# Graph convolution on one core: order, biases and first layer of the edge MLP changed

## What is computed

```
h   = relu(layernorm(x));  xp = h @ lin1                      # [12500, 128]
C   = 0.5 * (cos(edge_weight * pi / 10) + 1)                  # [212500]
W   = (ssp(edge_attr @ w1 + b1) @ w2 + b2) * C[:, None]       # [212500, 128], ssp(v) = softplus(v) - log 2
agg = segment_sum(xp[src] * W, dst)                           # [12500, 128]
out = x + ssp(agg @ lin2 + lin2_b) @ lin + lin_b
```

## Time and profile before

| | us |
|---|---|
| median of 3 runs | 2164.73 |
| lowest, highest run | 2164.29, 2168.45 |
| span of the profiled execution | 2162.6 |
| TensorE matmul busy | 1804.4 (83%) |
| VectorE busy | 1433.5 (66%) |
| ScalarE busy | 636.2 (29%) |
| GpSimd busy | 1626.7 (75%) |

### The profile page before, as it was taken

One profiled execution on the slowest core, in us unless ns is written; L12 is line 12 of the kernel. 1 busy time (PEld: TensorE's weight loads), 2 busy tenths in 40 slices (PEclk: granted clock), 3 DMA queues, 4 the chain that ended last, 5 costly groups with the idle time before them and its releaser, 6 DMA issues.

```text
span 2162.6 us, 28443 instructions
## 1 busy us (share of the span) xinstructions
PE 1804.4 (83%) x8534; PEld 1331.3 (62%) x8535; DVE 1433.5 (66%) x3688; ACT 636.2 (29%) x976; POOL 1626.7 (75%) x1742
## 2 busy tenths in 40 slices
PE   6888888888877888878888888888878888878887
PEld 6556666666655656656665666666656666655665
DVE  7867666666665666666666666666667666666665
ACT  6323232222222222222232222222322223222221
POOL 7877777777777777777777777777777777777775
PEclk9678787687787787887687877777778678788776
DMA  9322222222232222223232222222222222232221
GB/s 286 90 73 69 81 76 75 79 76 81 68 82 81 71 79 81 75 74 82 68 82 79 77 79 70 81 81 68 81 81 75 74 81 76 74 81 76 73 72 47
DMA packets 100170, 175.95 MB, mean 81 GB/s; under 512 B 29163, under 2 KB 67748, under 8 KB 94870
## 3 DMA queue, kind: packets, MB, share of 16 engines
q0 software_dynamic: 53152, 108.91, 18.0%
q1 hardware_dynamic: 46868, 65.22, 11.4%
HBM read 161.21 MB, written 12.80 MB: 80 GB/s over the span
## 4 chain that ended last, share of the span: by engine, by line
POOL 60%; issue 20%; PE 14%; DMA 3%; DVE 2%; DVEq 0%; ACT 0%; POOLq 0%; SPq 0%
POOL XG L307 59%; PE PW L619 4%; PE PA L631 4%; PE PX L605 3%; DMA XG<-xp_scratch,IX 3%; PE PW L617 1%; DVE SCR L403 1%; POOL TB L207 1%; DVE XG L509 1%; PE PF L648 0%; DVE MV L409 0%; PE PF L656 0%; PE PW L586 0%; DMA X<-x 0%; PE PX L573 0%
## 5 line engine op out<-in xcount | busy, mean ns | idle before, releaser
L307 POOL DMA_INDIRECT XG<-xp_scratch,IX x1661 | 1574.8, 948 | 507.4 <-issue 498.3
L371 ACT ACTIVATE TB<-TB 128x512 f32<-128x512 f32 x416 | 261.7, 629 | 1407.0 <-DVE TB L491 1406.9
L619 PEld LDWEIGHTS PW<-W,TB 128*128 128x128 f32 x3322 | 592.2, 251 | 21.4
L619 PE MATMUL PW<-W,TB 128*128 128x128 f32 x3322 | 594.5, 338 | 0.0
L509 DVE TENSOR_TENSOR XG<-PW,XG 128x512 f32<-128x512 f32 x416 | 286.2, 688 | 451.1 <-DMA XG<-xp_scratch,IX 448.1
L605 PE MATMUL PX<-AT,W 50*128 50x512 f32 x832 | 554.8, 752 | 7.1 <-DMA AT<-attr_t 7.1
L631 PEld LDWEIGHTS PA<-OH,XG 128*128 128x128 f32 x3322 | 544.4, 248 | 1.0 <-DVE XG L509 0.5
L631 PE MATMUL PA<-OH,XG 128*128 128x64 f32 x3322 | 543.3, 322 | 0.2 <-DVE AG L517 0.2
L617 PEld LDWEIGHTS PW<-BPB,ones 128*128 128x128 bf16 x416 | 41.3, 99 | 704.4 <-issue 649.6
L617 PE MATMUL PW<-BPB,ones 128*128 128x512 bf16 x416 | 195.2, 469 | 315.4 <-DVE XG L509 314.4
L491 DVE TENSOR_SCALAR TB<-PX,B 128x512 f32<-128x512 f32 x416 | 309.8, 745 | 202.9 <-PE PX L605 200.5
(11 more groups left out here) (73 smaller groups left out, 329.2 us busy)
## 6 DMA issues: line engine op xcount, KB each, us to landing
AT<-attr_t SPq DMA_DIRECT2D x103, 400.0 KB
XG<-xp_scratch,IX POOLq DMA_INDIRECT x1661, 2.5
X<-x SPq DMA_DIRECT2D x12, 512.0 KB, 7.4
xp_scratch<-XG SPq DMA_DIRECT2D x24, 256.0 KB, 4.4
out<-X SPq DMA_DIRECT2D x24, 256.0 KB, 5.2
IX<-src_t SPq DMA_DIRECT2D x1, 830.5 KB, 6.5
CC<-ew_t SPq DMA_DIRECT2D x1, 830.5 KB, 8.4
DI<-dst_t SPq DMA_DIRECT2D x1, 830.5 KB
```

The source lines that it names most:

```text
L307: e.indirect_dma_start(XG[q % XG_N][0:p, k * D:(k + 1) * D], None, xp, bass.IndirectOffsetOnAxis(ap=IX[0:p, t0 + k:t0 + k + 1], axis=0)).t ...
L371: e.activation(T[:, 0:w], T[:, 0:w], ACT.Exp).then_inc(s_ex, 1)
L619: ins = e.matmul(P[0:p, k * D:(k + 1) * D], TB[q % TB_N][:, k * TILE:k * TILE + p], W2[:, :], start=False, stop=(k == n - 1))
```

## The change

- b1 is a 51st row of W1, against a row of ones in AT (`one`, loaded once per buffer). VectorE's clamp with b1 goes.
- ssp is written as max(v, 0) + Ln(0.5 exp(-|v|) + 0.5): ScalarE takes |v| from PSUM, then Exp and Ln, and VectorE adds.
- W1 and AT are laid out twice, on partitions 0 to 50 and 64 to 114. Even quads of a load lie below, odd ones above. At every even step TensorE runs the first layer of quads q and q+1, in halves of 256 columns that take turns between the two halves of its rows. `PX` has four banks.
- b2 is laid out over 128 partitions once (`BB`), and ScalarE copies it into `PW` ahead of the second layer (from quad 2 on), which then adds to it; the bf16 matmul goes.
- The masks of a quad are one instruction without C; C goes into the multiply, which becomes four instructions of 128 columns, each waiting for its own gather.
- `PA` is one bank. The accumulate of q moves to step q+4 of VectorE, ahead of the multiply of q+1, and the scatter of q waits for the accumulate of q-1.
- SP issues three table loads per turn in place of two, and two loads per attribute buffer in place of one.

```diff
--- before.py
+++ after.py
@@ -52,11 +53,12 @@
...
-    XG_N, TB_N, X1_N, OH_N = 6, 4, 3, 3
+    XG_N, TB_N, X1_N, OH_N = 6, 4, 4, 3
...
@@ -85,14 +87,14 @@
...
-        W1 = sb("W1", [NG, D])
+        W1 = sb("W1", [ODD + NG + 1, D])
...
-        B1 = sb("B1", [128, 2])
+        BB = sb("BB", [128, QT, D])
...
@@ -106,7 +108,7 @@
-        AT = [sb(f"AT{i}", [NG, CHQ * QE]) for i in range(AT_N)]
+        AT = [sb(f"AT{i}", [ODD + NG + 1, CHQ // 2 * QE]) for i in range(AT_N)]
...
@@ -118,9 +120,9 @@
-        PA = [ps(f"PA{i}") for i in range(2)]
+        PA = ps("PA")
-        PN = PW + PA
+        PN = PW + [PA, PX[3]]
...
@@ -239,28 +243,38 @@
...
             tables = [(IX[:, :], src_t, s_ix), (CC[:, :], ew_t, s_tb),
-                      (B1[:, 0:1], b1.rearrange("(p a) -> p a", a=1), s_bs),
...
-                      (W1[:, :], w1, s_dx), (W2[:, :], w2, s_dx), (WI[:, :], win, s_dx),
+                      (W1[0:NG, :], w1, s_dx), (W1[NG:NG + 1, :], b1.rearrange("(a d) -> a d", a=1), s_dx),
+                      (W1[ODD:ODD + NG, :], w1, s_dx),
+                      (W1[ODD + NG:ODD + NG + 1, :], b1.rearrange("(a d) -> a d", a=1), s_dx), (W2[:, :], w2, s_dx), (WI[:, :], win, s_dx),
                       (DUE, due.rearrange("(a q) -> a q", a=1), s_dx), (L2[:, :], lin2, s_dx), (L3[:, :], lin, s_dx)]
+            tables += [(AT[i][r + NG:r + NG + 1, :], one, s_dx) for i in range(AT_N) for r in (0, ODD)]
             for c in range(NNC):
                 keep(c)
                 if c >= 3 and c % 2 and tables:
-                    for _ in range(2):
+                    for _ in range(3):
...
-                e0 = k * CHQ * QE
-                w = min(CHQ * QE, EDGES - e0)
...
-                e.dma_start(AT[k % AT_N][:, 0:w], attr_t[:, e0:e0 + w]).then_inc(s_at[k % AT_N], 16)
+                for r in range(2):
+                    A = AT[k % AT_N][ODD * r:ODD * r + NG, :]
+                    if k < NCH - 1:
+                        e.dma_start(A.rearrange("p (j e) -> p j e", e=QE),
+                                    attr_t[:, k * CHQ * QE:(k + 1) * CHQ * QE].rearrange(
+                                        "p (j r e) -> p r j e", r=2, e=QE)[:, r]).then_inc(s_at[k % AT_N], 16)
+                    else:
+                        for j in range(CHQ // 2):
+                            e0 = (k * CHQ + 2 * j + r) * QE
+                            w = min(QE, EDGES - e0)
+                            e.dma_start(A[:, j * QE:j * QE + w], attr_t[:, e0:e0 + w]).then_inc(s_at[k % AT_N], 16)
...
@@ -361,16 +375,28 @@
...
+            e.wait_ge(s_bb, 1)
             for i in range(STEPS):
                 q = i
                 if q < NQ:
                     t0, n, last = quad(q)
                     w = (n - 1) * TILE + last
                     T = TB[q % TB_N]
-                    e.wait_ge(s_cl, q + 1)
-                    e.activation(T[:, 0:w], T[:, 0:w], ACT.Exp).then_inc(s_ex, 1)
+                    e.wait_ge(s_x1, q + 1)
+                    if q >= TB_N:
+                        e.wait_ge(s_w, q - TB_N + 1)
+                    e.activation(T[:, 0:w], PX[q % X1_N][:, 0:w], ACT.Abs).then_inc(s_ab, 1)
+                    e.wait_ge(s_ab, q + 1)
+                    e.activation(T[:, 0:w], T[:, 0:w], ACT.Exp, scale=-1.0).then_inc(s_ex, 1)
                     e.wait_ge(s_ex, q + 1)
                     e.activation(T[:, 0:w], T[:, 0:w], ACT.Ln, scale=0.5, bias=HALF[:, :]).then_inc(s_ln, 1)
+                q = i - 1
+                if 2 <= q < NQ:
+                    t0, n, last = quad(q)
+                    p = last if n == 1 else TILE
+                    e.wait_ge(s_m, q - 1)
+                    e.activation(PW[q % 2][0:p, 0:n * D], BB[0:p, 0:n, :].rearrange("p k d -> p (k d)"),
+                                 ACT.Copy).then_inc(s_pb, 1)
...
@@ -438,7 +464,8 @@
...
-            e.wait_ge(s_bs, 64)
+            e.wait_ge(s_bs, 48)
+            e.tensor_copy(BB[:, :, :], BR[:, 0, 0:1, :].to_broadcast([128, QT, D])).then_inc(s_bb, 1)
...
@@ -454,13 +481,12 @@
...
-            e.tensor_scalar_add(B1[:, 1:2], B1[:, 0:1], -LN2)
...
@@ -479,42 +505,38 @@
...
-                    e.scalar_tensor_tensor(out=T[:, 0:w], in0=PX[q % X1_N][:, 0:w], scalar=B1[:, 1:2],
-                                           in1=T[:, 0:w], op0=ALU.add, op1=ALU.max).then_inc(s_h, 1)
-                q = i
-                if q < NQ:
-                    t0, n, last = quad(q)
-                    w = (n - 1) * TILE + last
-                    e.wait_ge(s_x1, q + 1)
-                    if q >= TB_N:
-                        e.wait_ge(s_w, q - TB_N + 1)
-                    e.tensor_scalar(TB[q % TB_N][:, 0:w], PX[q % X1_N][:, 0:w], B1[:, 0:1], CLAMP,
-                                    ALU.add, ALU.min).then_inc(s_cl, 1)
+                    e.scalar_tensor_tensor(out=T[:, 0:w], in0=PX[q % X1_N][:, 0:w], scalar=0.0,
+                                           in1=T[:, 0:w], op0=ALU.max, op1=ALU.add).then_inc(s_h, 1)
                 q = i - 3
                 if 0 <= q < NQ:
                     t0, n, last = quad(q)
                     if q >= OH_N:
                         e.wait_ge(s_sc, q - OH_N + 1)
-                    for k in range(n):
-                        p = last if k == n - 1 else TILE
-                        ins = e.tensor_scalar(OH[q % OH_N][0:p, k, :], WI[0:p, 0:WIN], REL[0:p, t0 + k:t0 + k + 1],
-                                              CC[0:p, t0 + k:t0 + k + 1], ALU.is_equal, ALU.mult)
-                    ins.then_inc(s_oh, 1)
-                    e.wait_ge(s_w, q + 1)
-                    for k in range(n):
-                        e.wait_ge(s_g[q % XG_N][k], 16 * (q // XG_N + 1))
                     p = last if n == 1 else TILE
                     assert n == 1 or last == TILE
-                    G = XG[q % XG_N][0:p, 0:n * D]
-                    e.tensor_tensor(G, PW[q % 2][0:p, 0:n * D], G, ALU.mult).then_inc(s_m, 1)
-                q = i - 5
+                    e.tensor_tensor(OH[q % OH_N][0:p, 0:n, :], WI[0:p, 0:WIN].unsqueeze(1).to_broadcast([p, n, WIN]),
+                                    REL[0:p, t0:t0 + n].unsqueeze(2).to_broadcast([p, n, WIN]),
+                                    ALU.is_equal).then_inc(s_oh, 1)
+                q = i - 4
                 if 0 <= q < NQ:
                     e.wait_ge(s_sc, q + 1)
                     if q:
                         e.wait_ge(s_ac, q)
                     base = e.value_load(BI[0:1, q:q + 1], min_val=0, max_val=NODES - 1)
                     A = AG[:, bass.ds(base, WIN)]
-                    e.tensor_tensor(A, A, PA[q % 2][:, 0:WIN], ALU.add).then_inc(s_ac, 1)
+                    e.tensor_tensor(A, A, PA[:, 0:WIN], ALU.add).then_inc(s_ac, 1)
+                q = i - 3
+                if 0 <= q < NQ:
+                    t0, n, last = quad(q)
+                    p = last if n == 1 else TILE
+                    e.wait_ge(s_w, q + 1)
+                    for k in range(n):
+                        e.wait_ge(s_g[q % XG_N][k], 16 * (q // XG_N + 1))
+                        G = XG[q % XG_N][0:p, k * D:(k + 1) * D]
+                        ins = e.scalar_tensor_tensor(out=G, in0=PW[q % 2][0:p, k * D:(k + 1) * D],
+                                                     scalar=CC[0:p, t0 + k:t0 + k + 1], in1=G,
+                                                     op0=ALU.mult, op1=ALU.mult)
+                    ins.then_inc(s_m, 1)
...
@@ -586,49 +608,60 @@
...
                 q = i
-                if q < NQ:
-                    t0, n, last = quad(q)
-                    w = (n - 1) * TILE + last
+                if q < NQ and q % 2 == 0:
                     k = q // CHQ
-                    e.wait_ge(s_at[k % AT_N], 16 * (k // AT_N + 1))
+                    e.wait_ge(s_at[k % AT_N], 32 * (k // AT_N + 1) + (32 if k == NCH - 1 else 0))
                     if q < X1_N:
                         e.wait_ge(s_re, NNC)
+                        e.wait_ge(s_xe, NNC)
                     else:
-                        e.wait_ge(s_h, q - X1_N + 1)
-                    o = (q % CHQ) * QE
-                    e.matmul(PX[q % X1_N][:, 0:w], W1[:, :], AT[k % AT_N][:, o:o + w], start=True,
-                             stop=True).then_inc(s_x1, 1)
+                        e.wait_ge(s_h, q - X1_N + 2)
+                    o = (q % CHQ) // 2 * QE
+                    _, n, last = quad(q + 1)
+                    w = [QE, (n - 1) * TILE + last]
+                    turns = [(0, 0), (0, 1), (1, 0), (1, 1)] if w[1] == QE else [(0, 0), (1, 0), (0, 1), (1, 1)]
+                    for half, r in turns:
+                        a = half * QE // 2
+                        b = min(a + QE // 2, w[r])
+                        if a < b:
+                            K = slice(ODD * r, ODD * r + NG + 1)
+                            ins = e.matmul(PX[(q + r) % X1_N][:, a:b], W1[K, :], AT[k % AT_N][K, o + a:o + b],
```

(33 more changed lines are left out.)

17 lines of the change are left out of this document (10 added, 7 removed).

## The result

| | before | after |
|---|---|---|
| median, us | 2164.51 (4 runs) | **2719.26** (4 runs, 2699.73 to 2723.62) |
| ratio | | 1.2544, 95% interval 1.2501 to 1.2588 |
| span of the profiled execution, us | 2162.6 | 2719.9 |
| mean granted clock of TensorE | 0.779 | 0.557 |

The kernel is 25% slower. The forecast of 2308 us had the sign and the circuit right, the share of half clock in it wrong, and so the size far too small. The time lies outside the range, in rival B. All times are medians of the runs that lie within 1.5% of the fastest run of their kernel; only e2b_address had others (2291.82 and 2295.31 us beside 2257.62 and 2280.96), and its trace is of the run of 2295.31.

What follows compares the result with a forecast made beforehand. It took GpSimd's gathers (5.01 us per quad) as the bound before, and afterwards one quad's round through the engines: 85.5 + 415 rounds of 5.28 (2191) + 10 + 20 = 2306.5 us span, say 2308; range 2159 to 2480.

Steps and rivals of the forecast that it cites:

- the circuit: Multiply, b2 copy, second layer, scatter, accumulate, next multiply: each quad goes round in 4.47 us at full clock, 6.09 at half.
- the share of half clock: Part of the quads with TensorE at half clock: half of them taken, giving 5.28 us per quad; bounds a quarter and all.
- rival B: The quad's round at half clock throughout, or halves not running together: 2673 us, from 2480 on; chance 0.15.
- sign named ahead: Expected in the profile: GpSimd waiting 100 us or more for scatters, some 400 VectorE waits before the accumulate, chain not through GpSimd.
- Rival C: The gathers stay the bound at about 5.0 us per quad: 2160 to 2195 us; chance 0.28 in all.
- not slower: Whole kernel with gathers still deciding: faster than before (2159 us) 0.08, or no change 0.10.
- start: Ahead of the rounds: the first multiply was taken to end at 85.5 us.
- tail: Behind the last multiply: hop, scatter, accumulate and last output chunk, taken as 10 us.
- the chunks' 20 us: Output-layer chunks, put in 25 times, sticking out of TensorE's free 2.58 us: 20 us, bounds 0 and 50.
- all at half clock: Every quad's round on TensorE at half clock: 6.09 us per quad, 2673 us in the sum; chance 0.15.
- The halves: First layer of two quads side by side on TensorE: 1.12 us a pair at full clock, 2.07 at half, within its wait.
- Masks: One two-input VectorE mask instruction may hold up gathers: 0.07 us per quad, up to 29 us, 0 if they miss.

Runs made afterwards that it cites:

- e2b_address: The changed kernel with the accumulate's address loaded ahead of the wait for the scatter: 2269.29 us, where the kernel before takes 2163.67.
- e1b_order: The changed kernel with the accumulate put behind the multiply again, all else kept: 2175.59 us, where the kernel before takes 2167.97.
- e3b_single: The changed kernel with each quad's first layer run alone at its own step, halves never side by side: 2791.28 us, where the kernel before takes 2163.67.
- b0_before: The kernel before, unchanged and timed again: 2168.03 us, ratio 1.0003.
- e4b_dummy: The changed kernel with useless bf16 matmuls in TensorE's gaps, in two thirds of the steps: 2282.88 us, where the kernel before takes 2163.67.
- e6b_memset: The kernel before with GpSimd's 6144-column memset cut up and moved earlier, on a slower chip: 2494.37 us, where the kernel before takes 2500.85.
- e3_single: The changed kernel with each quad's first layer run alone at its own step, on a slower chip: 2821.67 us, where the kernel before takes 2524.28.
- e1: The changed kernel with the accumulate put behind the multiply again, on a slower chip: 2539.38 us, where the kernel before takes 2524.28.
- e4: The changed kernel with useless bf16 matmuls in TensorE's gaps, on a slower chip: 2664.04 us, where the kernel before takes 2524.28.

## Why the prediction failed in size

**Right.** GpSimd bound the kernel before, with slack behind it, and the new order uses that slack up in one circuit. Nearly every sign named ahead is there: the waits by their releaser and count (401, 414, 634.1 us), no wait for a gather before the multiply, the chain through copy, second layer, scatter, accumulate and multiply; only the multiplies take 1.13 us, not 0.92. e1b_order shows that the order closes it. Rival C and the chance of 0.18 for "not slower" rested on a full-clock round of 4.47 us; it measured 4.76, and only 23 of after's 413 rounds ran at it.

**The links**, forecast against 1003.03 to 1009.47:

| link | forecast | measured |
|---|---|---|
| b2 copy with both hops | 0.78 | 0.61 + 0.14 + 0.02 = 0.77 |
| second layer and scatter, half clock | 3.51 | 3.65 |
| the same, full clock | 1.89 | 1.99 (e.g. 1023.12 to 1025.11) |
| scatter's end to accumulate | 0.74 | 1007.43 to 1008.18, 0.75 |
| accumulate | 0.14 | 0.14 |
| four multiplies | 0.92 (upper bound 1.15) | 1.13 |
| round, half / full clock | 6.09 / 4.47 | 6.44 / 4.76 |

The address load, which hid under the multiply before and was read from a single row at the end of the trace, came out to 0.01 us. The multiply was taken from the width of 128 columns in an instruction of another form; with the scalar and PSUM as input four of them take 1.13, near my upper bound.

**The step that failed is the share of half clock.** I argued from the busy share (75% against 83%) that there would be "no smaller share of half clock than before", and then took half of the quads, barely more than the 44% of the time that before's clock of 0.779 means. It is 0.557, that is 89% of the time. The mean round, (2709.99 − 83.6)/415 = 6.33 us from the end of the first multiply to that of the last, is nearly the half-clock round. In the sum, which used 5.28 us a round: the longer round at half share, (6.44 + 4.76)/2 − 5.28 = 0.32, makes 133 us; the share, 6.33 − 5.60 = 0.73, makes 303 us; start −1.9, tail 0, and the chunks' 20 us are in the mean round already. 2306.5 + 133 + 303 − 2 − 20 = 2720.5, the span (2719.9) but for rounding. Of the 303 some 270 are the share by itself, 0.39 × 1.68 us × 415; the rest is mostly what the chunks stick out.

Two steps led to the half. I put the clock in as a number read beside the circuit, with bounds of a quarter and all, but it moves with the circuit: 0.692 with the circuit open (e1b_order), 0.558 with it closed, and in e2b_address 0.62 us less in the round brought 1.09 us. By what rule the waiting and the clock hang together stays open, since e3b_single waits less and has 0.534. And against "all at half clock" I held that TensorE would be busy for 3.51 + 2.07 = 5.58 us on end and that from such a stretch the clock had risen; but the stretch in the earlier trace rows went from 1002 to 1009.6, 7.6 us. In after the engine ran on end from 997.34 to 1003.00 at half clock, and the clock did not rise. "All at half clock" had 0.15; its 2673 us were the nearest of the forecasts.

**The halves** run side by side, as forecast: two quads take 2.08 us at half clock (1000.92), the same as one quad in e3b_single (1004.32, 2.07). Undoing it costs 72 us (2791.28 against 2719.73 on another chip). The Trainium skill (TensorEngine Tiling (Array Packing), section Tiling Modes, Key Properties) lets tiles work in parallel, and these rows agree; of the drain between modes that it names no gap is to be seen, the pair at 1000.92 follows the scatter directly.

**Masks**: gathers 6.5 us longer in all where they are the bound (bounds 0 and 29), with masks and multiply changed together. The Trainium skill (GPSIMD Engine Reference, section Specifications) names contention with VectorE instructions of two SBUF inputs; the gathers' busy time in e1b_order and b0_before (1582.0 and 1575.5) goes that way, but no run tries such a mask alone.

## What to carry to other kernels

When an order or a wait is moved, follow one item from engine to engine until it comes back to the place it started from, add the links at both clock levels, and compare the slower sum with the pace of the engine that binds now. If the sum at half clock is above that pace and TensorE waits inside the circuit, don't carry over the clock of before: price the case that nearly all rounds run at half clock as a likely one, as 327 of 413 did here. Load addresses and issue waits that don't depend on the awaited result ahead of the wait; here the address load alone gave back 450 of 552 us.

## What the runs showed of the chip beyond that

- Useless work can pay: 437 us faster with 975 more bf16 matmuls recorded (277.0 us busy); the rounds keep their two lengths, and the clock is 0.835 against 0.558.
- A high busy share does not secure the clock: 87% gave 0.534 (e3b_single), 73% gave 0.835 (e4b_dummy) and 0.557 (after).
- Chips differ. On three of them the kernel before took 2501, 2524 and 2531 us. Its gathers are as short as ever (mean 947 ns in e6b_memset, 948 in b0_before), but engines wait for signals that the profile puts down as "remote", a kind of wait that no trace of a kernel on the other chips has:

```profile
DVE TB L495 <- remote: 782.7, 179, 15.7
POOL XG L311 <- remote: 255.8, 114, 3.7
```

  These are of e6b_memset, where the first should be TensorE's first layer. e3_single, bound by the circuit, is 1% slower on such a chip than on the others (2821.67 against 2791.28), the kernel before and e1 some 15 to 17%. e4 is 17% slower there (2664.04 against 2282.88), with the same circuit. The cause is open.
